# The odd layer-0 steps in three passes of rounded operands, and three chunks per tile scaled in PSUM by ScalarE

## The chip, the cores and the metric

The kernel runs on one core of a Trainium2 chip. The metric is the device time of one execution in microseconds (us). The core has five engines that run their own instruction streams in order and meet only at semaphores: TensorE (PE, matmuls; PEld is its weight load), VectorE (DVE), ScalarE (ACT), GpSimd (POOL) and SyncE (SP), which here only issues DMAs. SBUF is the working memory, PSUM holds what TensorE writes.

## The reference

The kernel computes three layers of feature crossing on x of shape (512, 64, 16), that is batch b, field f and element d:

```
x_vec = x
for W, b in ((W0, b0), (W1, b1), (W2, b2)):
    z     = einsum('bhd,bfd->bhfd', x_vec, x)         # outer product of fields, for every element
    x_vec = einsum('oc,bcd->bod', W, z as (b, h*f, d)) + b
    out  += [x_vec summed over d]                      # (512, 128) for each layer
return concatenate(out, axis=1)                        # (512, 384)
```

W0 is 128 x 4096 (64 times 64 field pairs), W1 and W2 are 128 x 8192. All is float32.

## The kernel before

**Tiling.** The batch is cut into 16 groups of 32 rows. A group has 4 tiles of 8 rows, and a tile has 128 columns (8 rows times 16 elements). A tile's layer 1 is cut into 16 chunks of 4 fields, so a group has 64 *positions* e = 0 to 63; position e is chunk c = e mod 16 of tile j = e div 16.

**Layer 0** uses that a pair of fields counts the same in both orders. A group needs 17 steps t = 0 to 16. For each, SP loads fields shifted by 2t into a slot of `z` (line 284), POOL multiplies the slot by the unshifted fields `xg` (line 337, "product t"), and PE adds W0's part times `z` into the PSUM bank `l0` (line 656, a float32 matmul of 512 columns). The last step, t = 16, has only 96 rows and is split into rounded parts (fp32r) by ACT (line 411) and DVE (line 542); line 652 is its matmul. The layer 0 of group n+1 is computed during group n: step t stands on PE behind the chunk at position `AHEAD_AT[t]` = 9, 11, 14, 17, 20, 23, 26, 29, 32, 34, 37, 40, 43, 46, 49, 52, 55. `z` has 9 slots; a slot is loaded again once PE has done the step that used it.

**Layer 1.** Its input is split into an upper rounded part `x1h` (ACT, line 431) and the rest `x1l` (DVE, line 559); W1 was split likewise at the start. A chunk is three rounded matmuls of 512 columns (`by_parts`, line 644: upper by upper, upper by lower, lower by upper) into one of four PSUM banks `y[c % 4]`. The bank then has to be multiplied, field by field, by the layer's own fields `x0t` and summed:

- chunks 1, 4, 7, 10, 13 (`HELPED`): ACT multiplies each quarter into SBUF `prod` (line 490), and POOL adds `prod` up (lines 346, 348);
- the other eleven (`SUMMED`): DVE multiplies and adds each quarter into `acc` in one instruction (line 584; line 582 for the first chunk).

At a tile's end POOL adds `acc` and folds the sum to `x2` (lines 354, 356, 359). PE may start the chunk at position e once the chunk at e-4 has left the bank.

**Layer 2** takes per tile two small matmuls (line 691), with a block-diagonal operand `bd` that DVE makes (line 551), and every fourth group 64 matmuls with W2 (line 679).

**What sets the order.** Each engine's stream is written out by hand, position by position, and runs strictly in that order. On ACT a position is: multiply (if helped), the layer-2 copies (lines 437, 439, at c = 13), the split of step 16 (position 50), then x1h and x0t for the next group (position 56). On DVE: add the chunk, `bd` at c = 11, the lower part of step 16 (position 51), x1l (positions 59 and, for tile 3, 4), the layer-0 sum (position 6). On POOL `PRODUCTS_AT` sets how many products stand before each step of a tile:

```
PRODUCTS_AT = ((2, 1, 1, 1, 1), (1, 1, 1, 1, 1), (1, 1, 1, 1, 0), (2, 0, 0, 0, 0))
...
products(0)                      # PRODUCTS_AT[j][0] products
combine(tile - 1, (j - 1) % 2)   # line 354 on
for h in range(1, HN):
    products(h)
    add_products(tile, h)        # waits for chunk HELPED[h] of this tile
```

So tile 0 holds products 0 to 5 of the next group, tile 1 holds 6 to 10, tile 2 holds 11 to 14, and products 15 and 16 stand at the head of tile 3, behind the addition for chunk 13 of tile 2 (position 45).

Of the kernel before, what the change touches and what calls it, by code (L numbers as in the profile page):

```python
# [13 lines left out]
O = 128  # L14
P = 128
# [22 lines left out]
ZSLOTS = 9  # L38
# [9 lines left out]
SN = CF * len(SUMMED)  # L48
# [14 lines left out]
AHEAD_AT = [9 + t * 46 // (ZT - 1) for t in range(ZT)]  # L63
LEFT_PARTS_AT = AHEAD_AT[-1] - 5
# [22 lines left out]
def cin_kernel(nc, x, w0, b0, w1, b1, w2, b2, out):  # L87
    with ExitStack() as ctx:
# [14 lines left out]
        w0t = sb("w0t", [P, ZT - 1, O])  # L103
        w0left = sb("w0left", [P, O], F32R)
        z = sb("z", [P, ZSLOTS, GROUP])
        zleft = sb("zleft", [P, GROUP], F32R)
# [54 lines left out]
        z_made = sem("z_made")  # L161
        left_made = sem("left_made")
# [12 lines left out]
        prod_made = sem("prod_made")  # L175
        pool_step = sem("pool_step")
# [54 lines left out]

        def tile_added(tile):

            return SN * tile + 2 * SN
# [152 lines left out]
        def _(act):  # L387
# [107 lines left out]
            for k, (what, r, bank) in enumerate(PREP):  # L495
                if what == "l0":
                    if r == ZT - 1:
                        left_parts(0)
                    continue
# [4 lines left out]
                if not parted(what, r):  # L504
                    nc.scalar.copy(w0t[:, 4 * r:4 * r + 4, :],
                                   y[bank][:].rearrange("p (t o) -> p t o", o=O)).then_inc(y_used[bank], 1)
                    continue
# [16 lines left out]
        def _(dve):  # L524
# [11 lines left out]
            nc.vector.tensor_scalar(b2d[:], b2c[:], float(D), None, ALU.mult).then_inc(bias_made, 1)  # L536

# [31 lines left out]
            def add_fields(tile, j, c):  # L569

                m = SUMMED.index(c)
                if m == 0:
                    dve.wait_ge(x2_made, x2_ready(tile - 2))
                dve.wait_ge(y_made, CHUNKS * tile + c + 1)
                for k in range(CF):
                    f = CF * c + k
                    to, of = acc[:, j % 2, k, :], y[c % YB][:, k * O:(k + 1) * O]
                    if m > 0 and k % 2 == 0:

                        dve.wait_ge(acc_step, SN * tile + (SN + CF * (m - 1) + k + 2))  # L580
# [31 lines left out]
            for k, (what, r, bank) in enumerate(PREP):  # L612
                if what == "l0":
                    if r == ZT - 1:
                        left_lower(0)
                    continue
                if not parted(what, r):
# [17 lines left out]
        def _(pe):  # L635
# [11 lines left out]
            def layer0(n, t):  # L647

                rows, slot = z_rows(t), zslot(t)
                if t == ZT - 1:  # L650
# [44 lines left out]
            def chunk(tile, j, c):  # L695
# [112 lines left out]
```

## Time and profile before

| | |
|---|---|
| median of 3 runs | 1136.26 us (1135.72 to 1136.55) |
| the profiled execution: its own time | 1133.84 us |
| the profiled execution: its span | 1132.0 us |
| PE busy | 1091.2 us (96%) |
| DVE busy | 866.7 us (77%) |
| POOL busy | 840.8 us (74%) |
| ACT busy | 450.3 us (40%) |

The profile is one execution. Busy time is an average over all stages. Matmul ends are modelled, so that PE reads as busy even where matmuls merely overlap; the distance from one matmul's start to the next tells more. In the table of 40 slices PE stands at 9 tenths or more from the third slice to the last but one. The granted TensorE clock is full (2.4 GHz) but for the first slices and the last. A group takes 62.67 us (from 397.73 to 460.40 us, for one), or some 77 us where the matmuls with W2 come in.

### The profile page before, as it was taken

What the parts mean: (1) busy time and instruction counts of PE and PEld (TensorE: products, weight loads), DVE (VectorE), ACT (ScalarE), POOL (GpSimd) and SP (SyncE); (2) the same over time, 40 slices, a digit from 0 to 9 for tenths busy, and PEclk for the clock granted to TensorE, in tenths of its full rate; (3) what the DMA queues carried; (4) which work ended last, traced back from release to release, by engine and by line L of the source; (5) the groups of instructions that cost most, each with busy time, mean ns of one, the idle gap of its engine ahead of it and who ended that gap; (6) DMA issues with size and microseconds to landing.
All of it is one profiled execution on the core that took longest, in us unless ns stands there. A gap on an engine that the chain in (4) does not pass through costs nothing.

```text
span 1132.0 us, 16831 instructions
## 1 busy us (share of the span) xinstructions
PE 1091.2 (96%) x4589; PEld 777.8 (69%) x4589; DVE 866.7 (77%) x3002; ACT 450.3 (40%) x1532; POOL 840.8 (74%) x762
## 2 busy tenths in 40 slices
PE   2899999999999999999999999999999999999996
PEld 2477666666678766666768676766667766666776
DVE  3356978888893888879794797978887588888990
ACT  2244434444341443435342343534343243443550
POOL 4766797979784797878876688787978479697561
PEclk9989999999999999999999999999999999999998
DMA  7861423314051241414142051423313133240000
GB/s 253 249 165 38 94 72 70 90 32 122 23 125 40 37 113 25 123 35 112 54 94 57 17 118 49 99 67 78 89 33 99 35 85 82 43 112 12 1 1 28
DMA packets 112350, 86.89 MB, mean 77 GB/s; under 512 B 75136, under 2 KB 75776, under 8 KB 112128
## 3 DMA queue, kind: packets, MB, share of 16 engines
q1 hardware_dynamic: 109376, 75.27, 27.7%
q10 hardware_dynamic: 2880, 10.55, 2.6%
q8 instruction: 36, 0.59, 0.2%
q14 instruction: 58, 0.48, 0.1%
HBM read 14.75 MB, written 0.79 MB: 14 GB/s over the span
## 4 chain that ended last, share of the span: by engine, by line
PE 83%; DVE 11%; DMA 3%; issue 2%; POOL 0%; ACT 0%; SPq 0%; POOLq 0%
PE y L644 54%; PE l L656 19%; DVE acc L584 8%; PE xt L679 5%; PE l2p L691 3%; DMA xg<-in_r_input_dram 2%; DVE bd L551 2%; DMA z<-xg 1%; DVE x1l L559 1%; PE l2p L668 1%; PE l L652 0%; PE xt L661 0%; PE y L733 0%; SPq L284 0%; DVE acc L582 0%
## 5 line engine op out<-in xcount | busy, mean ns | idle before, releaser
L584 DVE SCALAR_TENSOR_TENSOR acc<-y,x0t,acc 128x128 f32<-128x128 f32 x2560 | 698.7, 342 | 197.5 <-PE y L644 194.7
L490 ACT ACTIVATE prod<-y,x0t 128x128 f32<-128x128 f32 x1280 | 365.1, 368 | 604.1 <-PE y L644 569.8
L644 PE MATMUL y<-w1h,x1h 128*128 128x512 f32 x1024 | 507.2, 495 | 6.3 <-DVE acc L584 4.3
L644 PE MATMUL y<-w1h,x1l 128*128 128x512 f32 x1024 | 403.9, 394 | 0.0
L644 PE MATMUL y<-w1l,x1h 128*128 128x512 f32 x1024 | 403.4, 394 | 0.0
L348 POOL TENSOR_TENSOR pacc<-pacc,prod 128x512 f32<-128x512 f32 x192 | 247.4, 1288 | 187.8 <-ACT prod L490 187.8
L337 POOL TENSOR_TENSOR z<-z,xg 128x512 f32<-128x512 f32 (+1 forms) x272 | 352.6, 1302 | 25.7 <-DMA z<-xg 25.5
L644 PEld LDWEIGHTS y<-w1h,x1h 128*128 128x128 f32 x1024 | 193.2, 189 | 133.4 <-issue 61.5
L656 PE MATMUL l<-z,w0t 128*128 128x512 f32 x512 | 263.3, 596 | 3.8 <-POOL z L337 3.8
L644 PEld LDWEIGHTS y<-w1l,x1h 128*128 128x128 f32 x1024 | 193.4, 189 | 81.4 <-issue 54.3
L644 PEld LDWEIGHTS y<-w1h,x1l 128*128 128x128 f32 x1024 | 192.5, 188 | 43.7
L656 PEld LDWEIGHTS l<-z,w0t 128*128 128x128 f32 x512 | 95.6, 191 | 26.0 <-POOL z L337 3.8
L346 POOL TENSOR_TENSOR pacc<-prod 128x512 f32<-128x512 f32 x64 | 85.4, 1335 | 31.2 <-ACT prod L490 31.2
L354 POOL TENSOR_TENSOR pacc<-pacc,acc 128x512 f32<-128x512 f32 x64 | 83.0, 1297 | 4.2 <-DVE acc L584 3.3
L679 PEld LDWEIGHTS xt<-gram,w2t 128*128 128x128 f32 x512 | 63.7, 199 | 3.3 <-ACT sums L439 1.3
L679 PE MATMUL xt<-gram,w2t 128*128 128x128 f32 x512 | 64.0, 283 | 0.7 <-ACT sums L439 0.7
L551 DVE TENSOR_TENSOR bd<-x0t,own_half 128x256 f32<-128x256 f32 x64 | 62.1, 970 | 0.0
L582 DVE TENSOR_SCALAR acc<-y,x0t 128x128 f32<-128x128 f32 x192 | 54.9, 342 | 0.0
L356 POOL TENSOR_TENSOR pacc<-pacc 128x256 f32<-128x256 f32 x64 | 46.8, 731 | 5.0
L691 PE MATMUL l2p<-bd,x 64*128 64x260 f32 x256 | 45.5, 432 | 4.5 <-POOL x L359 4.5
L437 ACT COPY gram<-l2p 128x512 f32<-128x512 f32 x64 | 38.6, 603 | 5.0 <-PE l2p L691 5.0
L691 PEld LDWEIGHTS l2p<-bd,x 64*128 64x128 f32 x256 | 19.3, 184 | 27.8 <-issue 22.8
(50 smaller groups left out, 278.3 us busy)
## 6 DMA issues: line engine op xcount, KB each, us to landing
z<-xg SPq DMA_DIRECT2D x512, 128.0 KB, 2.4
xg<-in_r_input_dram SPq DMA_DIRECT2D x32, 128.0 KB, 3.8
w2t<-in_L_rec_W_dram ACTq DMA_DIRECT2D x8, 512.0 KB, 12.4
gram<-in_L_rec_W_dram ACTq DMA_DIRECT2D x8, 512.0 KB, 9.0
z<-xg SPq DMA_DIRECT2D x16, 192.0 KB
gram<-in_L_rec_W_dram ACTq DMA_DIRECT2D x1, 2048.0 KB, 7.9
out_dram<-z SPq DMA_DIRECT2D x4, 192.0 KB, 2.1
b1r<-in_L_rec_b_dram ACTq DMA_DIRECT2D x1, 64.0 KB, 9.8
```

The costliest lines, as they stand in the source:

```text
L337: nc.gpsimd.tensor_tensor(z[0:rows, slot, :], z[0:rows, slot, :], xg[0:rows, :], ALU.mult).then_inc(z_made, 1)
L346: nc.gpsimd.tensor_tensor(pacc[:], prod[:, 0], prod[:, 1], ALU.add).then_inc(pool_step, 1)
L348: nc.gpsimd.tensor_tensor(pacc[:], pacc[:], prod[:, h % HSLOTS], ALU.add).then_inc(pool_step, 1)
L354: nc.gpsimd.tensor_tensor(pacc[:], pacc[:], acc[:, slot], ALU.add).then_inc(pool_step, 1)
L490: last = nc.scalar.activation(prod[:, h % HSLOTS, k, :], y[c % YB][:, k * O:(k + 1) * O], ACT.Copy, scale=x0t[:, j, f:f + 1])
L551: nc.vector.tensor_tensor(bd[:, j % 2, 0:GRAM].rearrange("p (b f) -> p b f", f=F), x0t[:, j, :].unsqueeze(1).to_broadcast(shape), own_half ...
L582: ins = nc.vector.tensor_scalar(to, of, x0t[:, j, f:f + 1], None, ALU.mult)
L584: ins = nc.vector.scalar_tensor_tensor(out=to, in0=of, scalar=x0t[:, j, f:f + 1], in1=b1r[:] if m == 0 else to, op0=ALU.mult, op1=ALU.add)
L644: ins = nc.tensor.matmul(to, stationary, moving, start=(first and k == 0), stop=(last and k == 2))
L656: nc.tensor.matmul(l0[:], w0t[:, t, :], z[:, slot, :], start=(t == 0), stop=False).then_inc(z_used, 1)
L679: last = nc.tensor.matmul(l2, w2t[:, f, :], gram[:, f, :], start=(f == 0), stop=(f == F - 1))
L691: last = nc.tensor.matmul(l2p[:, k, 0:GRAM + HALF_B], x2[half, slot], bd[half, slot, :], start=True, stop=True)
```

## The change

**Odd steps by parts.** Steps 1, 3, ..., 15 (`PARTED`) no longer run as one float32 matmul. ACT rounds the product `z` into `zh` (fp32r) six positions ahead of the step, DVE subtracts to get the rest `zl` four positions ahead, and PE runs three rounded matmuls, as for a chunk. W0 is split for these steps at the start. The even steps stay as they were.

**Three chunks per tile scaled in place.** For chunks 3, 9 and 15 (in the last group 3, 6, 9 and 15) ACT multiplies the four quarters by `x0t` inside PSUM, and DVE then adds the whole bank to `acc` with one instruction of 512 columns, in place of four of 128. The five helped chunks stay on ACT and POOL, eight chunks stay on DVE.

**Slots.** `z` has 6 slots in place of 9; `zh` and `zl` have two each. POOL's stream and its table are not touched.

```
-ZSLOTS = 9
+ZSLOTS = 6
+PARTED = tuple(range(1, ZT - 1, 2))
+PN = len(PARTED)
+ZHSLOTS = 2
...
-SN = CF * len(SUMMED)
+SCALED = (3, 9, 15)
+SCALED_LAST = (3, 6, 9, 15)
...
+PART_UPPER_AT, PART_LOWER_AT = ([AHEAD_AT[t] - k for t in PARTED] for k in (6, 4))
...
# ACT
+            def part_upper(n, t):
+                i = PN * n + PARTED.index(t)
+                act.wait_ge(z_made, ZT * n + t + 1)
+                if i >= ZHSLOTS:
+                    before = i - ZHSLOTS
+                    act.wait_ge(z_used, ZT * (before // PN) + PARTED[before % PN] + 1)
+                nc.scalar.copy(zh[:, i % ZHSLOTS, :], z[:, zslot(t), :]).then_inc(zh_made, 1)
...
                     if c in HELPED:
                         multiply(tile, j, c)
+                    elif c in scaled_in(tile):
+                        scale(tile, j, c)
...
+                    if e in PART_UPPER_AT and kind != "last":
+                        part_upper(n + 1, PARTED[PART_UPPER_AT.index(e)])
                     if e == LEFT_PARTS_AT and kind != "last":
                         left_parts(n + 1)
...
+            def scale(tile, j, c):
+                act.wait_ge(y_made, CHUNKS * tile + c + 1)
+                for k in range(CF):
+                    f = CF * c + k
+                    of = y[c % YB][:, k * O:(k + 1) * O]
+                    last = nc.scalar.activation(of, of, ACT.Copy, scale=x0t[:, j, f:f + 1])
+                last.then_inc(y_scaled, 1)
# DVE
+            def part_lower(n, t):
+                i = PN * n + PARTED.index(t)
+                dve.wait_ge(zh_made, i + 1)
+                nc.vector.tensor_tensor(zl[:, i % ZHSLOTS, :], z[:, zslot(t), :],
+                                        zh[:, i % ZHSLOTS, :].bitcast(F32), ALU.subtract).then_inc(zl_made, 1)
...
+                if c in scaled_in(tile):
+                    dve.wait_ge(y_scaled, scaled_at(tile, c))
+                    dve.wait_ge(acc_step, added(tile, SUMMED[m - 1]))
+                    to = acc[:, j % 2].rearrange("p k o -> p (k o)")
+                    nc.vector.tensor_tensor(to, y[c % YB][:], to, ALU.add).then_inc(acc_step, 1)
+                    return
# PE
+                if t in PARTED:
+                    i = PARTED.index(t)
+                    pe.wait_ge(zl_made, PN * n + i + 1)
+                    by_parts(l0[:], zh[:, (PN * n + i) % ZHSLOTS, :], zl[:, (PN * n + i) % ZHSLOTS, :], w0h[:, i, :],
+                             w0l[:, i, :], t == 0, False, False).then_inc(z_used, 1)
+                    return
```

The positions that follow: ACT's `zh` copies stand at 5, 11, 17, 23, 28, 34, 40, 46, and DVE's `zl` subtractions at 7, 13, 19, 25, 30, 36, 42, 48, each behind that position's chunk. In the streams, names are those of the program and y0 to y3 are the four banks.

ACT of the kernel before, from chunk 13 of tile 2 (position 45, bank y1) to the split of step 16 (position 50); waits are named in brackets:

```order
L490 ACTIVATE prod<-y1,x0t 128x128 [waits pool_step,y_made]
L490 ACTIVATE prod<-y1,x0t 128x128 x3
L437 COPY gram<-l2p 128x64x8 [waits l2p_made]
L439 COPY sums<-l2p 128x8
L490 ACTIVATE prod<-y1,x0t 128x128 [waits pool_step,y_made,x0t_made]
L490 ACTIVATE prod<-y1,x0t 128x128 x3
L411 CAST zleft<-z 96x512 [waits z_used,z_made]
```

The second group of y1 is chunk 1 of tile 3. The same stretch of the changed kernel:

```order
L561 ACTIVATE prod<-y1,x0t 128x128 [waits pool_step,y_made]
L561 ACTIVATE prod<-y1,x0t 128x128 x3
L495 COPY gram<-l2p 128x64x8 [waits l2p_made]
L497 COPY sums<-l2p 128x8
L460 CAST zh<-z 128x512 [waits z_used,z_made]
L550 ACTIVATE y3<-y3,x0t 128x128 [waits y_made]
L550 ACTIVATE y3<-y3,x0t 128x128 x3
L561 ACTIVATE prod<-y1,x0t 128x128 [waits pool_step,y_made,x0t_made]
L561 ACTIVATE prod<-y1,x0t 128x128 x3
L469 CAST zleft<-z 96x512 [waits z_used,z_made]
```

The copy of step 15 to `zh`, which waits for POOL's product, and the scaling of chunk 15 (bank y3) now stand between chunk 13 and chunk 1.

DVE of the kernel before, from the end of chunk 15 of tile 2 (bank y3) through chunk 0 (y0), 2 (y2) and 3 (y3) of tile 3:

```order
L584 SCALAR_TENSOR_TENSOR acc<-y3,x0t,acc 128x128 [waits acc_step]
L584 SCALAR_TENSOR_TENSOR acc<-y3,x0t,acc 128x128
L584 SCALAR_TENSOR_TENSOR acc<-y0,x0t,b1r 128x128 [waits y_made,x2_made,x0t_made]
L582 TENSOR_SCALAR acc<-y0,x0t 128x128 x3
L584 SCALAR_TENSOR_TENSOR acc<-y2,x0t,acc 128x128 [waits acc_step,y_made]
L584 SCALAR_TENSOR_TENSOR acc<-y2,x0t,acc 128x128
L584 SCALAR_TENSOR_TENSOR acc<-y2,x0t,acc 128x128 [waits acc_step]
L584 SCALAR_TENSOR_TENSOR acc<-y2,x0t,acc 128x128
L584 SCALAR_TENSOR_TENSOR acc<-y3,x0t,acc 128x128 [waits acc_step,y_made]
```

The same stretch of the changed kernel:

```order
L657 TENSOR_TENSOR acc<-y3,acc 128x512 [waits acc_step,y_scaled]
L672 SCALAR_TENSOR_TENSOR acc<-y0,x0t,b1r 128x128 [waits y_made,x2_made,x0t_made]
L670 TENSOR_SCALAR acc<-y0,x0t 128x128 x3
L614 TENSOR_TENSOR zl<-z,zh 128x512 [waits zh_made]
L672 SCALAR_TENSOR_TENSOR acc<-y2,x0t,acc 128x128 [waits acc_step,y_made]
L672 SCALAR_TENSOR_TENSOR acc<-y2,x0t,acc 128x128
L672 SCALAR_TENSOR_TENSOR acc<-y2,x0t,acc 128x128 [waits acc_step]
L672 SCALAR_TENSOR_TENSOR acc<-y2,x0t,acc 128x128
L657 TENSOR_TENSOR acc<-y3,acc 128x512 [waits acc_step,y_scaled]
```

Chunks 15 and 3 are one addition each, which waits for ACT's scaling, and the subtraction for step 15 stands between chunks 0 and 2.

## Rows read from the trace of the kernel before

**Rows 1.** The page's chain that ended last, by engine.

```profile
PE 83%; DVE 11%; DMA 3%; issue 2%; POOL 0%; ACT 0%; SPq 0%; POOLq 0%
```

**Rows 2.** The chain over one group: start us, us, what.

```profile
397.73 3.00 PE y L644 x12
...
405.15 0.86 PE l L656 x2
...
408.96 0.64 PE l2p L691 x4
...
412.02 2.09 PE y L644 x9
...
454.55 0.67 DVE acc L584 x3
...
460.40 3.00 PE y L644 x12
```

**Rows 3.** Timeline, positions 45 to 64: start us, us, engine, line, [idle before <-releaser].

```profile
444.10 1.14 ACT L490 ACTIVATE prod<-y,x0t 128x128 f32<-128x128 f32 x4 [2.64 <-PE y L644]
...
445.32 1.29 POOL L348 TENSOR_TENSOR pacc<-pacc,prod 128x512 f32<-128x512 f32 x1 [2.50 <-ACT prod L490]
...
446.34 1.13 DVE L584 SCALAR_TENSOR_TENSOR acc<-y,x0t,acc 128x128 f32<-128x128 f32 x4 [0.43 <-PE y L644]
446.57 2.53 POOL L337 TENSOR_TENSOR z<-z,xg 128x512 f32<-128x512 f32 x2
...
447.38 0.34 DVE L584 SCALAR_TENSOR_TENSOR acc<-y,x0t,b1r 128x128 f32<-128x128 f32 x1
447.53 1.02 PE L656 MATMUL l<-z,w0t 128*128 128x512 f32 x2
...
449.13 0.62 ACT L411 CAST zleft<-z 96x512 fp32r<-96x512 f32 x1 [0.21 <-POOL z L337]
449.29 2.16 DVE L584 SCALAR_TENSOR_TENSOR acc<-y,x0t,acc 128x128 f32<-128x128 f32 x8 [0.79 <-PE y L644]
...
452.27 5.47 DVE L584 SCALAR_TENSOR_TENSOR acc<-y,x0t,acc 128x128 f32<-128x128 f32 x20
...
460.40 0.47 PE L644 MATMUL y<-w1h,x1h 128*128 128x512 f32 x1 [0.25 <-DVE acc L584]
```

**Rows 4.** Busy time in one group's stretch: us, PE, PEld, DVE, ACT, POOL (instructions), clock, DMA.

```profile
397.73:460.40 62.67, 62.42 (x246) 43.25 (x246) 52.98 (x185) 26.64 (x96) 51.83 (x46) 1.00 0.32 76
```

**Rows 5.** Groups of instructions by form: busy us, mean ns; then bd's line, min/median/max ns.

```profile
L542 DVE TENSOR_TENSOR zleft<-z,zleft 32x512 fp32r<-32x512 f32 x16 | 12.1, 755 | 3.2 <-ACT zleft L411 2.8
L622 DVE TENSOR_TENSOR w1l<-y,w1h 128x512 fp32r<-128x512 f32 x16 | 10.9, 691 | 19.4 <-ACT w1h L509 19.4
...
L551 DVE TENSOR_TENSOR bd<-x0t,own_half x64: 409/1026/1423, 72.3 to 1100.8; 128x256 f32<-128x256 f32 x64
```

**Rows 6.** Timeline of the preparation, and of positions 14 and 16 in a group.

```profile
24.51 21.03 SPq L284 DMA_DIRECT2D z<-xg  x32
...
44.63 3.77 POOL L337 TENSOR_TENSOR z<-z,xg 128x512 f32<-128x512 f32 x3 [1.50 <-DMA z<-xg]
...
44.67 5.21 ACTq L396 DMA_DIRECT2D gram<-in_L_rec_W_dram  x8
...
411.21 1.13 DVE L584 SCALAR_TENSOR_TENSOR acc<-y,x0t,acc 128x128 f32<-128x128 f32 x4 [1.07 <-PE y L644]
...
413.95 1.26 POOL L337 TENSOR_TENSOR z<-z,xg 128x512 f32<-128x512 f32 x1
```

**Rows 7.** The page's DMA issues: KB each, median us from issue to landing.

```profile
z<-xg SPq DMA_DIRECT2D x512, 128.0 KB, 2.4
```

**Rows 8.** The chain at the preparation's end, and in the last group, one tile apart.

```profile
45.58 7.60 DMA z<-xg
...
1064.48 0.73 DVE bd L551
...
1076.59 0.75 DVE bd L551
```

More of the change, by code:

```diff
@@ L102, in cin_kernel @@
         gram = sb("gram", [P, F, QB])
-        w0t = sb("w0t", [P, ZT - 1, O])
+        w0t = sb("w0t", [P, ZT - 1 - PN, O])
+        w0h = sb("w0h", [P, PN, O], F32R)
+        w0l = sb("w0l", [P, PN, O], F32R)
         w0left = sb("w0left", [P, O], F32R)
         z = sb("z", [P, ZSLOTS, GROUP])
+        zh = sb("zh", [P, ZHSLOTS, GROUP], F32R)
+        zl = sb("zl", [P, ZHSLOTS, GROUP], F32R)
         zleft = sb("zleft", [P, GROUP], F32R)
@@ L161, in cin_kernel @@
         z_made = sem("z_made")
+        zh_made = sem("zh_made")
+        zl_made = sem("zl_made")
         left_made = sem("left_made")
@@ L220, in weights @@
                 return of_w1[:, r, :], y[bank][:]
+            if r < W0_STEPS - 1:
+                of_w0 = w0h if of_w1 is w1h else w0l
+                return of_w0[:, 2 * r:2 * r + 2, :], y[bank][:].rearrange("p (t o) -> p t o", o=O)[:, PARTED[0]:4:2, :]
             return w0left[rows, :], y[bank][rows, 0:O]
@@ L224, in z_rows, with in_last, scaled_in, add_steps @@
             return P if t < ZT - 1 else ZCOPIES * ZLAST
-        def tile_added(tile):
-            return SN * tile + 2 * SN
+        def in_last(tile):
+            return isinstance(tile, int) and tile >= LAST_TILES
+        def scaled_in(tile):
+            return SCALED_LAST if in_last(tile) else SCALED
+        def add_steps(scaled, upto):
+            return sum(1 if c in scaled else CF for c in SUMMED if c <= upto)
+        SN = add_steps(SCALED, CHUNKS)
+        def added_before(tile):
+            if in_last(tile):
+                return SN * LAST_TILES + SN + add_steps(SCALED_LAST, CHUNKS) * (tile - LAST_TILES)
+            return SN * tile + SN
+        def added(tile, c):
+            return added_before(tile) + add_steps(scaled_in(tile), c)
+        def tile_added(tile):
+            return added_before(tile + 1)
+        def scaled_at(tile, c):
+            before = len(SCALED) * tile
+            if in_last(tile):
+                before = len(SCALED) * LAST_TILES + len(SCALED_LAST) * (tile - LAST_TILES)
+            return before + scaled_in(tile).index(c) + 1
         def x2_ready(tile):
@@ L503, in _ @@
                 act.wait_ge(prep_made, turned_in(PREP[:k]) + 1)
[L504 to L507, printed above, removed]
+                if what == "w0" and r < W0_STEPS - 1:
+                    nc.scalar.copy(w0t[:, 2 * r:2 * r + 2, :],
+                                   y[bank][:].rearrange("p (t o) -> p t o", o=O)[:, 1 - PARTED[0]:4:2, :])
                 part, of = weights(w1h, what, r, bank, slice(0, z_rows(ZT - 1)))
@@ L573, in add_fields @@
                     dve.wait_ge(x2_made, x2_ready(tile - 2))
+                if c in scaled_in(tile):
[4 more added lines that the diff above has]
+                    return
                 dve.wait_ge(y_made, CHUNKS * tile + c + 1)
+                after_scaled = m > 0 and SUMMED[m - 1] in scaled_in(tile)
                 for k in range(CF):
@@ L577, in add_fields @@
                     to, of = acc[:, j % 2, k, :], y[c % YB][:, k * O:(k + 1) * O]
-                    if m > 0 and k % 2 == 0:
-                        dve.wait_ge(acc_step, SN * tile + (SN + CF * (m - 1) + k + 2))
+                    if after_scaled and k == 0:
+                        dve.wait_ge(acc_step, added(tile, SUMMED[m - 1]))
+                    elif m > 0 and not after_scaled and k % 2 == 0:
+                        dve.wait_ge(acc_step, added(tile, SUMMED[m - 1]) + (k + 2 - CF))
                     if m == 0 and k > 0:
@@ L602, in body @@
                         own_rows(n * TILES + j, j)
+                    if e in PART_LOWER_AT and kind != "last":
+                        part_lower(n + 1, PARTED[PART_LOWER_AT.index(e)])
                     if e == LEFT_LOWER_AT and kind != "last":
@@ L613, in _ @@
                 if what == "l0":
+                    if r in PARTED:
+                        part_lower(0, r)
                     if r == ZT - 1:
                         left_lower(0)
-                    continue
-                if not parted(what, r):
                     continue
@@ L654, in layer0 @@
                     return
+                if t in PARTED:
[4 more added lines that the diff above has]
+                    return
                 pe.wait_ge(z_made, ZT * n + t + 1)
-                nc.tensor.matmul(l0[:], w0t[:, t, :], z[:, slot, :], start=(t == 0), stop=False).then_inc(z_used, 1)
+                nc.tensor.matmul(l0[:], w0t[:, t // 2, :], z[:, slot, :], start=(t == 0), stop=False).then_inc(z_used, 1)
             def turn_fields():
@@ L701, in chunk @@
                 else:
-                    value = SN * tile + (SN + CF * SUMMED.index(before) + CF) - (SN if late else 0)
-                    pe.wait_ge(acc_step, value)
+                    pe.wait_ge(acc_step, added(tile - 1 if late else tile, before))
                 cols = slice(j * P, (j + 1) * P)
```

6 lines of the change are left out of this document (5 added, 1 removed).

## The prediction

> **What bounds the kernel now.** I read the chain that ended last first: 83% of it is PE, 11% DVE [rows 1]. The same chain over one group [rows 2] gives PE's prices and says where DVE comes in. A chunk costs 2.09 / 3 = 0.70 us, a float32 step of layer 0 costs 0.86, the pair for layer 2 costs 0.64. One group start to the next is 62.67 us. Sixty-four chunks (44.6), sixteen steps (13.7) and four pairs (2.6) make 60.9 of that; step 16, the turn of the fields and waits share the other 1.8. So PE sets the pace nearly everywhere. The exception begins at 454.55: from there to the group's end the chain runs through DVE's additions, and PE's first chunk of the next group starts when DVE lets it [rows 2, 3]. In one group DVE is busy 52.98 of 62.67 us, POOL 51.83, ACT only 26.64 [rows 4]. ACT looks free, but a share does not tell whether its work can be done when it is wanted.
>
> For that I read the timeline around positions 45 to 51 [rows 3]. ACT takes chunk 13 of tile 2 (position 45) at 444.10. POOL adds it from 445.32, and only then makes products 15 and 16, as two of 1.26 us from 446.57. So product 15 is there at 447.83, product 16 at 449.10. The copy for step 16 (449.13) already waits 0.21 us for POOL there. DVE takes chunk 15 at 446.34 and starts the next tile at 447.38.
>
> **The change, part by part.**
>
> *PE.* An odd step becomes three rounded matmuls of 512 columns. A chunk is three of the same, so I take 0.70 in place of 0.86: 0.16 us less, 8 steps per group, 15 groups, 19.2 us. Nothing hides it where PE sets the pace.
>
> *DVE.* Per tile three chunks go from four instructions (5.47 / 20 = 0.273 each, 1.09 a chunk) to one addition of 512 columns. The nearest row is line 622 with the same columns and one PSUM input, 0.69 [rows 3, 5]. That frees 0.40 us each. Per group eight subtractions of 512 columns come in, both inputs in SBUF. Bounds: 0.69 (line 622, one input in PSUM) or 0.76 (line 542, 32 rows) alone, and up to 1.01 more beside POOL, for `bd`, also from two SBUF inputs, takes 0.41 at best, 1.03 in the median and 1.42 at worst [rows 5]; its long cases start while POOL is inside an instruction. I take 0.69 + 0.62 = 1.3. Per group DVE gains 12 x 0.40 = 4.8 and pays 8 x 1.3 = 10.4: it goes from 53 to some 58.6 us, still below the period, but close.
>
> The Trainium skill bears on this. Its "GPSIMD Engine Reference", section "Key points", says that GpSimd shares its SBUF interfaces with VectorE and that the two get in each other's way when a VectorE instruction has two SBUF inputs. The spread of `bd` agrees. By that rule each subtraction waits for POOL whenever POOL is busy; without it all eight would cost 0.69 to 0.76, and the sum below would be some 7 us smaller.
>
> *ACT.* Twelve scalings of 1.14 (as line 490) and eight copies of 0.62 (as line 411) per group are 18.6 us: 26.6 becomes 45 of 62.67. The volume fits. The place does not. ACT's copy for step 15 stands at position 46, ahead of the scaling of chunk 15, and waits for product 15. That product stands on POOL behind the addition for chunk 13, which ACT itself has just made, and POOL's stream is unchanged. Hence, with the kernel before's times: ACT is done with chunk 13 and the layer-2 copies at about 445.8, waits until 447.85, copies until 448.45, scales chunk 15 until 449.55. DVE, which waits for this with everything of tile 3 behind it, adds it from 449.6 to 450.3. Before, it was ready for tile 3 at 447.38: 2.9 us later.
>
> *What that delays.* PE's position 51 uses chunk 15's bank. Step 14 starts at 447.53, so 51 would start at 447.53 + 0.86 + 0.70 - 0.16 = 448.9; it now starts at 450.4, a stall of 1.5 us. From there DVE sets the end as it did before, from chunk 0 of tile 3 to chunk 12, whose bank the next group needs first. Before, that stretch lasted 460.40 - 447.38 = 13.0 us. Now two chunks are additions (-0.8). One subtraction is added; POOL's fold of the tile starts as DVE frees it at 450.3 and its first instruction ends at 451.6, just after the subtraction wants to start, so +0.95. The idle 0.79 before chunk 2 is gone. And DVE waits for the scaling of chunk 9, since ACT at position 56 first does chunk 7, x1h and x0t: I take +0.6 (bounds 0 and 1.4, the whole latency of a scaling). Sum about 0: the next group starts 2.9 late; I take 2.7, as the chunks that DVE finds waiting run without gaps.
>
> *What comes back.* In tile 0 the two subtractions (2.6) less the three chunks' gain (1.2) fill DVE's idle time, 1.07 of which stands before chunk 14 [rows 6], so DVE makes up nothing, and PE is late again by its own work from there. It gains 0.16 at steps 1, 3, 5, 7, 9 and 11 before the next position 45: 0.96. Steps 13 and 15 lie inside the delayed stretch. Each period of 62.67 (and of 77) therefore becomes 2.7 - 0.96 = 1.74 longer.
>
> *Slots.* With six, a load waits for the step six back. Step 0 ends at 406.0 [rows 2]; two issues at 21.03 / 32 = 0.66 and 2.4 us to land give 409.7, and POOL wants that slot at 413.95 [rows 6, 7]. Nothing, with 4 us in hand. SP is in order, but product 16 and so its next load of `xg` keep their place.
>
> *Preparation.* ACT's copy of step 13 now precedes its issue of W2's load (44.67, 5.21 us of issuing). It waits for product 13, the second of three from 44.63, so the load leaves some 3 us later, and the last copies with it. Against this, the transfer of step 16's slot, 7.60 us beside that load, may land sooner [rows 6, 8]. Bounds -3.5 and +3, I take +1.
>
> *Last group.* No layer 0 is left; DVE sets 1076.59 - 1064.48 = 12.1 us a tile [rows 8]. With four scaled chunks DVE frees 1.6 a tile, then PE's 16 x 0.70 + 0.64 = 11.8 comes next, and ACT's latency eats part. I take -1 (between -3 and +1.5).
>
> *Sum.* Fourteen periods from position 45 to position 45, 14 x 1.74 = 24.4; group 0 before its position 45, -0.96; the last stretch into group 15, +2.7; last group -1; preparation +1: +26.1. On the profiled execution's 1133.84 that is 1159.9. The median of the runs is 2.4 above that execution, so 1162 us.
>
> **Rivals.**
>
> *A, faster: the four banks absorb the wait at position 46.* Then only PE's saving is left, 1136.3 - 19.2 = 1117 us. For it: PE is 96% busy and ACT idle more than half of the time. Against it: it needs DVE's addition of chunk 15 to end before 448.9, so product 15 some 1.5 us earlier than 447.83, and on POOL nothing moved. That is the point from which it decides.
>
> *B, slower still: the subtractions collide with POOL throughout.* At 1.70 each DVE needs 53.0 - 4.8 + 13.6 = 61.8 us per group of work alone, and with the 2.9 us of waiting for chunk 15 a period is near 65: 14 x 2.3 and more over A's place, in all some 40 to 50 more than before, 1180 us. For it: POOL is busy 83% of a group [rows 4]. Against it: `bd`'s median is well under its worst.
>
> *C, a draw.* If the delayed stretch costs 1.0 in place of 2.7 (DVE's subtraction alone at 0.7, no wait for chunk 9, and PE's own slack at the group's end taking the rest), the steps give it all back: 1133 to 1142.
>
> *The three passes are no cheaper than float32.* Then 0.96 does not come back per period: 1175. The rows for chunks leave this little room.
>
> **How the numbers follow.** My forecast, own range 1146 to 1176: 0.72. A: 0.11. C: 0.10, with part of it on each side. B and the last together: 0.07. What a measurement here can tell from no change is about 0.2%, 2.3 us. Faster is A and a little of C, 0.13; same 0.04; slower 0.83. The range that leaves out A, the fastest of C and most of B is 1133 to 1178.
>
> **What would show it.** In the profile after: ACT's copy to `zh` at position 46 waits about 2 us for POOL's product, once per group and not at the other seven; behind it the scaling of chunk 15 starts some 2.5 us after its chunk was ready; PE waits for DVE's addition at position 51; group starts lie near 64.4 us apart; subtractions are between 0.7 and 1.7 us, long where POOL is busy. Odd steps at 0.70 on PE. I am wrong if group starts lie under 62 us apart, if the wait at position 46 is short because POOL's product comes earlier, or if PE's wait at 51 is there but the next group starts no later, which would mean that the stretch to the group's end has slack that I took for DVE's work.

## The result and the profile after

The changed kernel takes 1163.41 us (median of 4 runs, 1162.78 to 1163.51), the kernel before 1136.40 beside it: a ratio of 1.0246, 95% interval 1.023 to 1.0261. The profiled span goes from 1132.0 to 1161.8 us. The forecast was 1162.

The chain that ended last, by engine, of the changed kernel; this answers to [rows 1]:

```profile
PE 70%; DVE 12%; ACT 5%; POOL 4%; issue 4%; DMA 3%; SPq 0%; ACTq 0%; DVEq 0%; POOLq 0%
```

PE's share falls from 83% to 70%. ACT and POOL, which were on the chain with 0%, now hold 9% of it.

The chain over the same group as in [rows 2] (start us, us, what), from one group start to the next:

```profile
409.45 7.37 PE y L734 x30
...
425.73 0.68 PE l L734 x3
426.41 2.04 PE y L734 x9
428.45 0.86 PE l L752 x2
429.31 2.09 PE y L734 x9
...
454.93 0.89 ACT prod L561 x3
455.88 1.30 POOL pacc L397
457.18 1.25 POOL z L386
458.98 1.12 ACT y L550 x4
...
461.84 0.88 DVE zl L614
...
464.58 1.39 DVE zleft L621
...
468.45 0.86 ACT y L550 x3
...
473.70 0.47 PE y L734
```

A group lasts 473.70 - 409.45 = 64.25 us; before it was 62.67. On PE an odd step (`l L734`) costs 0.68 against 0.86 of an even one (`l L752`), and the three chunks behind it 2.04 against 2.09: by these rows 0.23 less per odd step. Then, at 454.93, the chain leaves PE and runs through ACT's chunk 13, POOL's addition, POOL's product 15, ACT's scaling of chunk 15 and DVE's stream. It takes PE and ACT once more, for the scaling of chunk 9, and comes back to PE at the next group's start.

The timeline of that place, ACT, POOL and DVE, then PE's two waits; it answers to [rows 3]:

```profile
454.66 1.14 ACT L561 ACTIVATE prod<-y,x0t 128x128 f32<-128x128 f32 x4 [2.12 <-PE y L734]
...
455.88 1.30 POOL L397 TENSOR_TENSOR pacc<-pacc,prod 128x512 f32<-128x512 f32 x1 [1.90 <-ACT prod L561]
...
457.13 2.52 POOL L386 TENSOR_TENSOR z<-z,xg 128x512 f32<-128x512 f32 x2
...
458.45 0.62 ACT L460 CAST zh<-z 128x512 fp32r<-128x512 f32 x1 [2.11 <-POOL z L386]
...
458.98 1.11 ACT L550 ACTIVATE y<-y,x0t 128x128 f32<-128x128 f32 x4
...
460.12 0.69 DVE L657 TENSOR_TENSOR acc<-y,acc 128x512 f32<-128x512 f32 x1 [3.65 <-ACT y L550]
460.73 0.34 DVE L672 SCALAR_TENSOR_TENSOR acc<-y,x0t,b1r 128x128 f32<-128x128 f32 x1
460.87 0.50 PE L734 MATMUL y<-w1h,x1h 128*128 128x512 f32 x1 [1.28 <-DVE acc L657]
...
464.13 1.29 POOL L395 TENSOR_TENSOR pacc<-prod 128x512 f32<-128x512 f32 x1 [0.27 <-ACT prod L561]
...
464.58 1.38 DVE L621 TENSOR_TENSOR zleft<-z,zleft 32x512 fp32r<-32x512 f32 x1
...
466.02 0.50 PE L742 MATMUL l<-zleft,w0left 96*128 96x512 f32 x1 [0.22 <-DVE zleft L621]
```

ACT's copy for step 15 waits 2.11 us for POOL; DVE waits 3.65 us for the scaling queued behind that copy; PE waits 1.28 us for DVE at position 51.

One group's busy time (PE, PEld, DVE, ACT, POOL), against [rows 4]:

```profile
409.45:473.70 64.25, 62.38 (x254) 44.38 (x254) 54.35 (x157) 43.47 (x152) 54.51 (x46) 1.00 0.31 73
```

No engine's work reaches the 64.25 us: DVE grew by 1.4 only, ACT by 17. A load alone doesn't explain the longer group; whether the order does is what the experiments test.

The new instructions by form (busy us, mean ns, idle time ahead of them), beside [rows 5]:

```profile
L657 DVE TENSOR_TENSOR acc<-y,acc 128x512 f32<-128x512 f32 x196 | 135.4, 691 | 148.8 <-ACT y L550 142.1
L614 DVE TENSOR_TENSOR zl<-z,zh 128x512 fp32r<-128x512 f32 x128 | 122.9, 960 | 11.1 <-ACT zh L460 11.1
L621 DVE TENSOR_TENSOR zleft<-z,zleft 32x512 fp32r<-32x512 f32 x16 | 21.5, 1343 | 0.5
L460 ACT CAST zh<-z 128x512 fp32r<-128x512 f32 x128 | 81.3, 635 | 75.4 <-POOL z L386 73.7
```

An addition of a scaled chunk takes the 0.69 us that were expected, a subtraction 0.96 instead of 1.3, and the old instruction for `zleft`, which nobody changed, 1.34 instead of 0.76. The copies to `zh` waited 73.7 us for POOL's products.

In the last group, where no layer 0 is left, the chain of two tiles, against [rows 8]:

```profile
1092.56 1.14 ACT prod L561 x4
...
1105.23 1.14 ACT prod L561 x4
...
1106.92 1.02 ACT y L550 x4
```

The same pattern comes back 12.67 us later; a tile took 12.11 before. ACT's product for chunk 13 and its scaling of chunk 15, with the layer-2 copies between, are now on the chain there.

### The profile page after: what moved, and what is told of

Read it like the earlier page. It is cut to its first block, busy times and chain, and to the rows that moved or that the text cites. A ratio compares the mean times of both kernels' runs of the same rounds, so it can differ in the third digit from the quotient of the medians.

```text
span 1161.8 us, 17673 instructions
## 1 busy us (share of the span) xinstructions
PE 1093.6 (94%) x4717; PEld 795.5 (68%) x4717; DVE 889.3 (77%) x2546; ACT 722.7 (62%) x2448; POOL 880.3 (76%) x762
## 4 chain that ended last, share of the span: by engine, by line
PE 70%; DVE 12%; ACT 5%; POOL 4%; issue 4%; DMA 3%; SPq 0%; ACTq 0%; DVEq 0%; POOLq 0%
PE y L734 46%; PE l L752 8%; PE l L734 6%; PE xt L775 5%; DVE acc L672 4%; ACT y L550 3%; PE l2p L787 3%; DMA xg<-in_r_input_dram 2%; POOL z L386 2%; DVE acc L657 2%; POOL pacc L397 2%; DVE zleft L621 2%; ACT prod L561 2%; DVE zl L614 1%; DVE acc L670 1%
## 5 line engine op out<-in xcount | busy, mean ns | idle before, releaser
L672 DVE SCALAR_TENSOR_TENSOR acc<-y,x0t,acc 128x128 f32<-128x128 f32 x1776 | 489.0, 340 | 62.4 <-PE y L734 56.7
L734 PE MATMUL y<-w1h,x1h 128*128 128x512 f32 x1024 | 468.5, 458 | 27.3 <-DVE acc L657 19.1
L734 PE MATMUL y<-w1h,x1l 128*128 128x512 f32 x1024 | 402.7, 393 | 0.0
L734 PE MATMUL y<-w1l,x1h 128*128 128x512 f32 x1024 | 401.9, 392 | 0.0
L386 POOL TENSOR_TENSOR z<-z,xg 128x512 f32<-128x512 f32 (+1 forms) x272 | 376.5, 1391 | 24.1 <-DMA z<-xg 23.9
L734 PEld LDWEIGHTS y<-w1h,x1h 128*128 128x128 f32 x1024 | 193.0, 189 | 153.1 <-DVE acc L672 44.0
L550 ACT ACTIVATE y<-y,x0t 128x128 f32<-128x128 f32 x784 | 219.2, 347 | 71.6 <-PE y L734 71.5
L657 DVE TENSOR_TENSOR acc<-y,acc 128x512 f32<-128x512 f32 x196 | 135.4, 691 | 148.8 <-ACT y L550 142.1
L734 PEld LDWEIGHTS y<-w1l,x1h 128*128 128x128 f32 x1024 | 193.4, 189 | 54.5 <-issue 25.4
L734 PEld LDWEIGHTS y<-w1h,x1l 128*128 128x128 f32 x1024 | 192.5, 188 | 43.0
L752 PE MATMUL l<-z,w0t 128*128 128x512 f32 x256 | 132.4, 598 | 2.2 <-POOL z L386 2.2
L614 DVE TENSOR_TENSOR zl<-z,zh 128x512 fp32r<-128x512 f32 x128 | 122.9, 960 | 11.1 <-ACT zh L460 11.1
L460 ACT CAST zh<-z 128x512 fp32r<-128x512 f32 x128 | 81.3, 635 | 75.4 <-POOL z L386 73.7
L734 PE MATMUL l<-zh,w0h 128*128 128x512 f32 x128 | 53.1, 415 | 4.6 <-DVE zl L614 4.4
L752 PEld LDWEIGHTS l<-z,w0t 128*128 128x128 f32 x256 | 47.8, 191 | 12.1 <-issue 3.0
```

The lines of the kernel that those rows point to most:

```text
L386: nc.gpsimd.tensor_tensor(z[0:rows, slot, :], z[0:rows, slot, :], xg[0:rows, :], ALU.mult).then_inc(z_made, 1)
L550: last = nc.scalar.activation(of, of, ACT.Copy, scale=x0t[:, j, f:f + 1])
L614: nc.vector.tensor_tensor(zl[:, i % ZHSLOTS, :], z[:, zslot(t), :], zh[:, i % ZHSLOTS, :].bitcast(F32), ALU.subtract).then_inc(zl_made, 1)
L657: nc.vector.tensor_tensor(to, y[c % YB][:], to, ALU.add).then_inc(acc_step, 1)
L672: ins = nc.vector.scalar_tensor_tensor(out=to, in0=of, scalar=x0t[:, j, f:f + 1], in1=b1r[:] if m == 0 else to, op0=ALU.mult, op1=ALU.add)
L734: ins = nc.tensor.matmul(to, stationary, moving, start=(first and k == 0), stop=(last and k == 2))
```

## The experiments

Theory 1: the copy for step 15 waits for POOL with the scaling of chunk 15 queued behind it; either half alone is cheap, both together are not. Theory 2: DVE has too much to do, or collides with POOL all over. Theory 3: the three passes save nothing.

The table has the medians, the ratio to the kernel before measured beside it with its 95% interval, and, from the starts of PE's chunks, by how much a stretch of positions grew against the kernel before: the period as a mean of groups 1 to 13, group 0 up to position 45, and the last group.

| kernel | us | ratio | period (0-45, 45-55, 55-60, 60-0') | group 0 | last |
|---|---|---|---|---|---|
| changed kernel | 1163.41 | 1.0246 [1.023, 1.0261] | +1.60 (-1.13, +1.66, +1.08, 0) | +1.99 | +1.04 |
| scaling alone | 1142.71 | 1.0069 [1.0046, 1.0092] | +0.31 (-0.15, 0, 0, +0.47) | +2.11 | +1.08 |
| scaling 3 and 15 alone | 1134.84 | 1.0008 [0.9995, 1.002] | -0.10 (-0.10, 0, 0, 0) | +1.20 | -0.15 |
| parts alone | 1120.94 | 0.987 [0.9845, 0.9895] | -1.02 (-1.12, -0.44, +0.55, 0) | +0.96 | -0.13 |
| product early | 1121.40 | 0.9876 [0.9855, 0.9897] | -1.27 (-1.31, -0.42, +0.28, +0.18) | +1.50 | +1.11 |
| copy behind | 1143.85 | 1.0073 [1.0052, 1.0095] | +0.25 (-1.12, +0.40, +0.98, 0) | +1.55 | +1.15 |
| chunk 15 on DVE | 1122.95 | 0.9895 [0.9881, 0.9909] | -1.04 (-1.12, -0.45, +0.54, 0) | +1.30 | +1.19 |
| parts, product early | 1131.85 | 0.9974 [0.9965, 0.9983] | -0.30 (-1.13, -0.45, +1.28, 0) | +0.79 | -0.09 |
| the same, `zleft` earlier | 1119.61 | 0.9862 [0.9847, 0.9877] | -1.13 (-1.13, -0.11, +0.11, 0) | +0.68 | -0.09 |
| parts, `zleft` earlier | 1120.27 | 0.9866 [0.9849, 0.9882] | -1.09 (-1.15, -0.06, +0.12, 0) | +0.75 | -0.06 |
| inner groups scaled, early | 1117.49 | 0.9846 [0.9833, 0.986] | -1.27 (-1.28, -0.45, +0.30, +0.15) | +0.20 | -0.30 |
| the same, 3 and 15 | 1118.78 | 0.9854 [0.9839, 0.9869] | -1.27 (-1.13, -0.43, +0.30, 0) | -0.13 | -0.16 |

**Scaling alone.** The kernel before with the change's scaling, its float32 steps and nine slots kept (this leaves PARTED out):

```diff
 (before.py)
+SCALED = (3, 9, 15)
+SCALED_LAST = (3, 6, 9, 15)
+                    elif c in scaled_in(tile):
+                        scale(tile, j, c)
```

> The kernel before, with the in-place scaling of three chunks per tile alone (float32 layer-0 steps, nine slots). Theory 1 (the changed kernel loses because ACT's copy for step 15 at position 46 waits for POOL's product and holds up chunk 15's scaling): that wait is not in here, DVE is eased by 4.8 us a group, so the stretch to a group's end is set by PE again; group starts 61.4 to 62.2 us apart, 1122 to 1134 us in all. Rival (the way through ACT and back to DVE, some 1.4 us longer per scaled chunk, is itself what costs): group starts above 62.7 us apart, 1137 us or more.

Measured: 1142.71 us, with a period of 62.98. That is the rival's range, not theory 1's. Positions 45 to 60 are unmoved: without a copy for step 15 the scaling of chunk 15 delays nobody. The 0.31 per group arises at the group's end. The timeline of DVE and PE there:

```profile
400.17 0.69 DVE L623 TENSOR_TENSOR acc<-y,acc 128x512 f32<-128x512 f32 x1 [0.73 <-ACT y L524]
...
404.55 0.47 PE L698 MATMUL y<-w1h,x1h 128*128 128x512 f32 x1 [0.71 <-DVE acc L638]
```

The scaling of chunk 9 of tile 3 stands on ACT behind `x1h` and `x0t`; DVE waits 0.73 us for it, and PE 0.71 at the next group's start. Fourteen of these, a later start (+3.0), group 0 and the last group make up the 11.0 us by which PE's last chunk comes later in the profiled execution. That execution (1145.15 us) lies 2.4 above the median.

**Parts alone.** The changed kernel without scaling:

```diff
-SCALED = (3, 9, 15)
-SCALED_LAST = (3, 6, 9, 15)
+SCALED = ()
+SCALED_LAST = ()
```

> The changed kernel without any scaling in PSUM: odd steps in three passes, all eleven chunks of DVE as before. ACT still waits at position 46, but the chunk behind it is chunk 1 at position 49. DVE has some 60.7 us of work per group (53.0 plus 8 subtractions of 0.96), more than in the changed kernel (56 us). Theory 1: no chunk of DVE hangs on the wait; DVE's load sets tiles 3 and 0, group starts 63 to 64.5 us apart, 1140 to 1160 us, below the changed kernel. Rival (the subtractions' load on DVE and their collisions with POOL set the period): DVE is fuller than in the changed kernel, so slower than it, above 1165 us.

Measured: 1120.94 us, much faster than either side expected, though DVE is busy for 978.8 us in it, against 889.3 in the changed kernel. That refutes theory 2 as the main cause, and theory 3: PE keeps 1.12 us by position 45. Scaling costs +0.31 alone and parts -1.02; their sum is -0.71, and the change has +1.60. So 2.3 us per period arise only where the two stand together. That fits theory 1; the next three runs test it.

**Product early.** The changed kernel, with POOL making product 15 ahead of the addition for chunk 13 of tile 2 instead of behind it:

```diff
-PRODUCTS_AT = ((2, 1, 1, 1, 1), (1, 1, 1, 1, 1), (1, 1, 1, 1, 0), (2, 0, 0, 0, 0))
+PRODUCTS_AT = ((2, 1, 1, 1, 1), (1, 1, 1, 1, 1), (1, 1, 1, 1, 1), (1, 0, 0, 0, 0))
```

> The changed kernel with POOL's product 15 one place earlier, ahead of the addition for chunk 13 of tile 2, where POOL stood idle for 1.9 us. Nothing else differs. Theory 1: ACT's copy at position 46 no longer waits, PE's wait at position 51 goes, and a period loses most of the 2.7 us: 61.5 to 62.5 us, 1122 to 1138 us. Rival (DVE's load and collisions with POOL): within 6 us of 1163.

Measured: 1121.40 us, some 40 less than the changed kernel and just under the expected range, by the place of one instruction per group. The timeline of ACT and DVE at that place:

```profile
442.29 0.67 ACT L460 CAST zh<-z 128x512 fp32r<-128x512 f32 x1
444.01 0.69 DVE L657 TENSOR_TENSOR acc<-y,acc 128x512 f32<-128x512 f32 x1 [1.45 <-ACT y L550]
...
448.49 0.68 DVE L621 TENSOR_TENSOR zleft<-z,zleft 32x512 fp32r<-32x512 f32 x1
```

The copy has no wait left, DVE's fell from 3.65 to 1.45, PE's at position 51 is gone, and `zleft` is back at 0.68.

**Copy behind.** The changed kernel with ACT's copy for step 15 one position later, behind the scaling of chunk 15; POOL's order stays:

```diff
+PART_UPPER_AT[-1] += 1
```

> The changed kernel with ACT's copy for step 15 one position later, that is behind the scaling of chunk 15 in place of ahead of it; POOL is untouched and ACT still waits for the product, but with nothing of DVE's behind it. Theory 1: chunk 15's addition ends near 448.3 on the earlier clock in place of 450.3, ahead of the 448.9 at which PE wants its bank; 61.5 to 62.7 us a period, 1122 to 1140 us. If instead the product's lateness itself matters (through step 15 on PE), it stays above 1150. Rival of DVE's load: within 6 us of 1163.

Measured: 1143.85 us, between the two ranges, so the expectation was only half met. The stall at position 51 is gone (45-51 is -0.23), but the stretch behind it grew. The timeline of DVE, POOL and PE:

```profile
450.45 2.54 POOL L387 TENSOR_TENSOR z<-z,xg 128x512 f32<-128x512 f32 x2
...
452.80 1.98 DVE L615 TENSOR_TENSOR zl<-z,zh 128x512 fp32r<-128x512 f32 x1
...
452.93 1.30 POOL L404 TENSOR_TENSOR pacc<-pacc,acc 128x512 f32<-128x512 f32 x1
...
454.84 0.50 PE L735 MATMUL l<-zh,w0h 128*128 128x512 f32 x1 [0.55 <-DVE zl L615]
...
456.09 1.29 POOL L396 TENSOR_TENSOR pacc<-prod 128x512 f32<-128x512 f32 x1 [0.17 <-ACT prod L562]
...
456.65 1.28 DVE L622 TENSOR_TENSOR zleft<-z,zleft 32x512 fp32r<-32x512 f32 x1
```

The subtraction for step 15 takes 1.98 us and `zleft` 1.28 because POOL's late instructions lie on them. The order on ACT is one cost of the late product, the place of POOL's work against DVE's subtractions a second.

**Chunk 15 on DVE.** The changed kernel with the copy's victim taken away:

```diff
-SCALED = (3, 9, 15)
+SCALED = (3, 9)
```

> The changed kernel with chunk 15 back on DVE in all but the last group (chunks 3 and 9 stay scaled); POOL and ACT's copy at position 46 are untouched, so ACT still waits some 2 us there. Theory 1 (the wait costs only because chunk 15's scaling, and DVE behind it, stand behind it): periods 61.4 to 62.0 us as with no scaling at all (61.62), 1119 to 1128 us. Rival (the wait on ACT costs by itself, through chunk 1's product and the copy of step 16 behind it): periods above 63 us, 1145 us or more.

Measured: 1122.95 us. The copy still waits as in the changed kernel (72 us over the run for POOL). The timeline of ACT there:

```profile
445.51 0.62 ACT L460 CAST zh<-z 128x512 fp32r<-128x512 f32 x1 [2.11 <-POOL z L386]
```

No scaling that DVE wants is queued behind it, and the period is that of the parts alone. What still stands behind the wait, chunk 1's product and the cast for step 16, comes later at no cost to the period.

**Scaling chunks 3 and 15 alone.** As scaling alone, without chunk 9 and without the last group:

```diff
-SCALED = (3, 9, 15)
-SCALED_LAST = (3, 6, 9, 15)
+SCALED = (3, 15)
+SCALED_LAST = ()
```

> Scaling alone, of chunks 3 and 15 only, and none in the last group (float32 steps as before). With chunk 9 scaled too the period was 62.98 us, 0.31 above the kernel before, because DVE waits 0.7 us at the group's end for chunk 9, whose scaling stands on ACT behind x1h and x0t. Theory: without chunk 9 that wait is gone and the period is 62.3 to 62.7 us, 1131 to 1137 us. Rival (each scaled chunk costs by its longer way): 62.8 us or more, 1138 us or more.

Measured: 1134.84 us. The +0.47 at the group's end and the +1.08 of the last group are gone, which gives them to chunk 9 and to the last group's scaling. By the starts of PE's chunks, scaling of these two chunks by itself is worth 0.10 us per period; the median can't be told from that of the kernel before.

**Parts, product early.** Both edits, no scaling:

```diff
 (parts alone)
-... (1, 1, 1, 1, 0), (2, 0, 0, 0, 0))
+... (1, 1, 1, 1, 1), (1, 0, 0, 0, 0))
```

> Odd steps in three passes, no scaling, and product 15 one place earlier on POOL. If scaling is worth nothing once the wait is gone, the period is that of the kernel with scaling and the early product (61.35 us) or below, and the end is shorter by 1 us, as the last group loses 1.1 us by scaling: 1117 to 1120 us. If scaling eases the group's end, 61.5 to 61.7 us a period, 1119 to 1122 us.

Measured: 1131.85 us, 11 more than the parts alone and not as expected: an early product that was worth some 40 us with scaling costs 11 without. All of it is in positions 55 to 60. The timeline there:

```profile
451.77 1.29 POOL L395 TENSOR_TENSOR pacc<-prod 128x512 f32<-128x512 f32 x1 [0.88 <-ACT prod L561]
...
451.86 1.75 DVE L621 TENSOR_TENSOR zleft<-z,zleft 32x512 fp32r<-32x512 f32 x1
...
453.66 0.50 PE L742 MATMUL l<-zleft,w0left 96*128 96x512 f32 x1 [0.43 <-DVE zleft L621]
```

`zleft` starts 0.09 us after a POOL instruction, takes 1.75 us, and PE's step 16 waits for it. POOL's own instruction keeps its 1.29. Is that the collision, or too much work on DVE? The next two runs are one and the same edit in two kernels.

**`zleft` one position earlier, product early.**

```diff
-LEFT_LOWER_AT = AHEAD_AT[-1] - 4
+LEFT_LOWER_AT = AHEAD_AT[-1] - 5
```

> The parts without scaling and with the product made early, and VectorE's lower part of the last, short step (zleft) one position earlier, after the third chunk of tile 3 instead of the fourth. Theory of the collision: in the kernel without this edit (1131.85 us) zleft takes 1.73 us, lying on GpSimd's product of 1.29 us at the same moment; one position earlier it would fall into GpSimd's idle stretch of 0.88 us, take 0.7 to 0.9 us, the wait of the last step on TensorE (0.43 us) would go, and the time would be 1116 to 1123 us. Theory of the load (VectorE has too much work without the scaling, wherever it stands): zleft becomes no shorter and the time stays at 1129 to 1133.

Measured: 1119.61 us, 12 less, with the same work on every engine. POOL and DVE:

```profile
447.41 0.46 POOL L408 TENSOR_TENSOR x<-pacc 128x128 f32<-128x128 f32 x1
...
447.80 0.68 DVE L621 TENSOR_TENSOR zleft<-z,zleft 32x512 fp32r<-32x512 f32 x1
...
448.75 1.29 POOL L395 TENSOR_TENSOR pacc<-prod 128x512 f32<-128x512 f32 x1 [0.88 <-ACT prod L561]
```

`zleft` lies in POOL's idle stretch but for its first 0.07 us and takes 0.68. So the 12 us were the collision.

**`zleft` one position earlier, product late.** The same line in the kernel with parts alone.

> The same move of zleft by one position, in the kernel with the parts alone and the product where the change has it (1120.94 us). There GpSimd combines its sums just at the earlier moment. Theory of the collision: zleft goes from 0.95 us to 1.4 to 1.8 us and the time rises to 1125 to 1133 us, the opposite sign of the same edit in the other kernel. A rule that the earlier place is better for TensorE in any case: 1120 us or less in both.

Measured: 1120.27 us, the other sign did not come. `zleft` became shorter here too, and POOL longer:

```profile
447.70 0.69 DVE L621 TENSOR_TENSOR zleft<-z,zleft 32x512 fp32r<-32x512 f32 x1
...
447.86 1.12 POOL L405 TENSOR_TENSOR pacc<-pacc 128x256 f32<-128x256 f32 x1
```

POOL's instruction takes 0.74 us where nothing lies on it, as in the parts alone (row 447.84 in the last section); here it started 0.16 us after `zleft` and waited for it. The expectation failed because it took DVE for the one that always waits. Here POOL started second, and it had the time. Against the parts alone (1120.94 us) the time is unchanged within the intervals, so the earlier place by itself is worth nothing that these runs can tell; the rival's 1120 or less was missed by 0.3 us, which doesn't decide on it.

**Inner groups scaled, product early.** Product early, with scaling in groups 1 to 14 only:

```diff
         def scaled_in(tile):
-            return SCALED_LAST if in_last(tile) else SCALED
+            return SCALED if TILES <= tile < LAST_TILES else ()
```

> The kernel with product 15 earlier, and scaling in groups 1 to 14 alone. Group 0 (where ACT also copies W2's transposes) and the last group lost some 1 us each where chunks were scaled; without it there: period 61.35 us as before, 1118.5 to 1120 us, 1.5 to 3 us below the 1121.4 of the kernel with scaling everywhere. Rival (those losses come from the split steps or the preparation): 1121 us or more.

Measured: 1117.49 us, the lowest median, 1.0 below the expected range: below the kernel before by 1.5% and below the changed one by some 46 us. Group 0 up to position 45 falls from +1.50 to +0.20 and the last group from +1.11 to -0.30. Group 0, now unscaled with the early product, has the collision of the parts with the early product: `zleft` takes 1.73 us there and 0.68 in the other groups.

**The same with chunks 3 and 15.** SCALED = (3, 15) in that kernel.

> The fastest kernel so far (scaling in the fourteen inner groups only, product early; 1117.49 us) with chunks 3 and 15 scaled, and chunk 9 not. If the wait for chunk 9's scaling at the end of a group (0.15 us of shift per group there) is what the third scaled chunk costs: 1114 to 1116.5. If VectorE, with 0.4 us more of work per tile, gets into GpSimd's way or late for tile 3: 1118 to 1126.

Measured: 1118.78 us, with the same period (-1.27). The first expectation did not come; the time lies in the second's range, but with the period the same its mechanism shows no cost. The 0.15 us at the group's end are gone and so is the 0.15 more that PE won back by position 45: a delay that was absorbed anyway. The intervals of the two overlap, so they can't be told apart.

## Why the prediction was right, point by point

*PE's three passes.* Forecast 0.16 us per odd step. By the rows of the chain it is 0.23: the step itself saves 0.18 and the chunks behind it 0.05, which the prediction did not count. By the starts of PE's chunks, a finer measure, it is 0.20 at each of steps 3 to 11, and some 0.1 is left for step 1. The six steps give -1.13 by position 45; forecast -0.96.

*ACT's wait at position 46.* Forecast about 2 us, measured 2.11, in the order described. DVE was to be ready for tile 3 2.9 us later; measured against position 45 on PE, it is 2.8 later (460.73 - 453.66 against 447.38 - 443.10). PE's stall at position 51: forecast 1.5, measured 1.28. That the other seven copies do not wait was wrong: the one for step 9 waits 1.8 us in 11 of 15 groups, the one for step 13 some 0.55. The longest other wait on ACT in this group:

```profile
437.42 0.62 ACT L460 CAST zh<-z 128x512 fp32r<-128x512 f32 x1 [1.77 <-POOL z L386]
```

PE shows no wait behind it, so the sum did not need it.

*The group's end.* Forecast +2.7, measured +1.66 + 1.08 = +2.74. Its parts were less good. The stretch on DVE was to stay at 13.0 us, and it did: 473.70 - 460.73 = 12.97. The subtraction there was put at 0.95 and took 0.96. Two terms were off and cancelled: the wait for the scaling of chunk 9 was put at 0.6 and is under 0.2 in the changed kernel, where DVE is late itself (0.73 where scaling stands alone); and `zleft`, which the prediction did not list among what could change, grew by 0.6.

*The subtractions.* Forecast 1.3 on average, 0.96 measured, inside the bounds. Several stand where POOL is idle (0.68). Their length outside the delayed stretch does not decide the time: up to position 45 PE gains 1.13 us here and 1.12 with the parts alone, where they average 1.17. Without any waiting for POOL the sum was to be some 7 us smaller. The terms that it gives make that 3 to 4, the one subtraction of the delayed stretch at 0.69 to 0.76 in place of 0.95 in 15 stretches.

*Group 0 and the last group* are where the prediction was wrong in sign: -0.96 and -1 were forecast, +1.99 and +1.04 came, 5 us in all. For the last group the term that failed is that DVE's freed 1.6 us a tile outweigh ACT's latency: ACT's product for chunk 13 and its scaling of chunk 15 stand on the chain, a tile takes 12.67 us in place of 12.11, and no kernel without scaling there lost time. In group 0 the step that failed is that PE sets the pace there. The runs with scaling show +1.2 to +2.1 and those without -0.13 to +0.96, so scaling is worth something over 1 us of the miss of 2.95. It can't be told more closely, since three kernels with the same instructions up to there (parts, product early, and the last two of the table) lie 0.9 apart. What keeps group 0 of the parts from -0.96 was not tried; in the changed kernel the chain there runs through the first loads and POOL's first products.

*Slots.* Six are enough, as forecast: POOL's idle time ahead of the products that is ended by a load is 23.9 us in the whole run, 25.5 with nine.

*Preparation.* Forecast +1, measured +0.6; over the kernels it lies between +0.6 and +3.0, so one profile doesn't fix it.

*The sum.* 15 stretches of +2.73, 14 of -1.13, +1.99, +1.04 and +0.58 are 28.8 us, PE's shift at its last position; forecast 26.1. The medians differ by 27.0, since the profiled execution of the kernel before lay 2.4 us below the median that it was forecast from. That the forecast of 1162 came within 1.4 us is in part luck. The delayed stretch, 41 us of the sum, was right in mechanism and size; the 5 us missed in group 0 and the last group were offset in part by 2.4 us more from the three passes, and by that profiled execution, which lay below its median where the changed kernel's lay at its own.

*The rivals.* A, a wait that the banks absorb, needed product 15 to come 1.5 us earlier. With that edit the time is 1121.40 us, where A put 1117: the point from which it decides was named rightly. B, collisions throughout, did not occur, but its mechanism did: it set apart the two runs with the early product and no scaling, on `zleft`. C wanted 1.0 us for the delayed stretch, and it is 2.74. That the three passes are no cheaper is refuted by the same -1.13.

## What to carry to other kernels

When a copy or a cast is added to an engine that looks idle, look up when its input is made, and what stands behind it in that engine's order: here 2.1 us of waiting on ScalarE cost nothing with no work for VectorE behind it, and 2.6 us per group with one scaling behind it (the changed kernel against chunk 15 on DVE). Two cures were worth some 40 us each: to make the product earlier, or to take the scaling out from behind the wait. To move the copy behind the scaling gave half of that. Of two edits made together, try each alone: the parts gained 1.3%, the scaling cost 0.7%, and the two together cost 2.5%.

## What the runs showed of the hardware

In these runs a VectorE subtraction with two SBUF inputs (`zl`, `zleft`) and a GpSimd instruction exclude each other nearly for their whole length, and the one that starts second pays. In the parts alone, for one more stretch of the timeline:

```profile
443.48 2.53 POOL L386 TENSOR_TENSOR z<-z,xg 128x512 f32<-128x512 f32 x2
...
445.45 1.16 DVE L614 TENSOR_TENSOR zl<-z,zh 128x512 fp32r<-128x512 f32 x1 [0.25 <-ACT zh L460]
...
445.97 1.80 POOL L403 TENSOR_TENSOR pacc<-pacc,acc 128x512 f32<-128x512 f32 x1
...
447.84 0.74 POOL L405 TENSOR_TENSOR pacc<-pacc 128x256 f32<-128x256 f32 x1
...
448.66 0.46 POOL L408 TENSOR_TENSOR x<-pacc 128x128 f32<-128x128 f32 x1
448.71 0.95 DVE L621 TENSOR_TENSOR zleft<-z,zleft 32x512 fp32r<-32x512 f32 x1
```

`zleft` ends 0.54 us after POOL's instruction here (449.66 and 449.12), 0.54 in the changed kernel (465.96 and 465.42), 0.55 in the parts with the early product (453.61 and 453.06) and 0.55 with the copy behind (457.93 and 457.38), whatever it had waited. Alone it takes 0.68. So its length goes from 0.68 to 1.75 us with nothing but the phase of the two engines. Over the twelve kernels of the table, 188 such subtractions started while POOL was idle, and all took 0.68 to 0.69 us. Of 1284 that started inside a POOL instruction, 1264 ended 0.54 to 0.62 us behind it.

Where POOL has two instructions one right behind the other, VectorE mostly gets in between: the `zl` above waits for the second product and POOL's next instruction then waits for `zl`, 1.80 us in place of some 1.29. It did so in 1042 of 1057 such places. The 15 others are all the subtraction for step 15 in the copy behind, which started 0.13 us ahead of the second POOL instruction and waited for both (1.98 us); what is different there was not tried. The additions of a scaled chunk, which have one input in PSUM, don't wait for POOL at all: 1320 of them took 0.68 to 0.69 us, 891 of these inside a POOL instruction.

The Trainium skill says this in "SBUF — State Buffer", section "SBUF: two separate sides": the shared pair of ports is an exclusive lock, held for the whole instruction by the one that starts first, and a VectorE instruction with two SBUF inputs takes part in it against a GpSimd instruction that reads SBUF. These rows agree, and the 1.12 us of POOL behind `zleft` shows that it holds in the other direction as well. Five of the 1284 don't fit by their starts: they began some 0.1 us after a POOL instruction and yet took 0.68 us.
